# Convolution taps of a Mamba-2 block read from the projection's PSUM bank, with the first decay sums moved to the head of TensorE's slot

## The reference

```python
zxbcdt = x @ W_in                       # z 512 columns, xBC 640 columns, dt 8 columns
lhs = transpose(xBC, (0, 2, 1))         # channels first
conv = conv_general_dilated(lhs, conv_w[:, None, :], padding=[(3, 0)], groups=640)
xBC = silu(transpose(conv, (0, 2, 1)) + conv_b)
# x_ssm, B, C are cut out of xBC; dt = softplus(dt + dt_bias)
def step(s, inp):                       # state, over the tokens
    s = s * dA_t[..., None, None] + dBx_t
    y = einsum('bhpn,bn->bhp', s, C_t)
# y = (y + D * x_ssm) * silu(z), RMS norm, times norm_weight, then y @ W_out
```

## Time and profile before

| | us |
|---|---|
| median of the three runs | 1308.08 |
| profiled execution, its own time | 1312.65 |
| span of the profiled execution | 1310.9 |
| busy TensorE matmul | 1062.4 (81%) |
| busy VectorE | 809.1 (62%) |
| busy GpSimd | 655.7 (50%) |
| busy ScalarE | 618.4 (47%) |

### The profile page before, as it was taken

How to read it: one execution, slowest core, us unless ns; L and a number is a source line. 1 busy time by engine, 2 the same in 40 slices (tenths; PEclk the granted TensorE clock), 3 DMA queues, 4 the chain that set the end, 5 groups by cost and what they waited for, 6 DMA issues and landing times. The chain is left out here.

```text
span 1310.9 us, 21923 instructions
## 1 busy us (share of the span) xinstructions
PE 1062.4 (81%) x6532; PEld 883.3 (67%) x6532; DVE 809.1 (62%) x1611; ACT 618.4 (47%) x1494; POOL 655.7 (50%) x593
## 2 busy tenths in 40 slices
PE   3747999999916788999999999989747999999900
PEld 3646999999914566766666666657536999999800
DVE  6974444444437898698989897875383444444434
ACT  1333555555513565556565656564333555555400
POOL 6913555555421465556565655567505555555300
PEclk9998999999966888788988888899868999999955
DMA  6861222222232111111111100000062222222178
GB/s 230 267 273 49 78 77 77 78 77 78 58 109 73 49 37 41 37 45 35 47 41 42 41 25 17 17 17 25 29 257 65 77 77 78 77 77 76 53 243 275
DMA packets 73242, 112.20 MB, mean 86 GB/s; under 512 B 10664, under 2 KB 60336, under 8 KB 71856
## 3 DMA queue, kind: packets, MB, share of 16 engines
q1 hardware_dynamic: 47888, 58.77, 13.2%
q0 software_dynamic: 13824, 37.77, 8.8%
q10 hardware_dynamic: 11424, 14.30, 3.2%
HBM read 66.76 MB, written 44.04 MB: 85 GB/s over the span
## 5 line engine op out<-in xcount | busy, mean ns | idle before, releaser
L399 POOL DMA_INDIRECT ys_d<-xs,row_of x144 | 142.0, 986 | 195.3 <-DVE xs L779 189.5
L768 DVE TENSOR_TENSOR xl<-pT,xh 128x256 fp32r<-128x256 f32 x144 | 61.1, 424 | 223.9 <-ACT xh L476 223.9
L394 POOL DMA_INDIRECT xs<-xn_d,token_of x144 | 139.8, 971 | 114.4 <-DVE token_of L753 71.2
L463 ACT ACTIVATE hs<-pH 128x512 f32<-128x512 f32 x144 | 86.0, 597 | 233.8 <-PE pH L581 233.8
L773 DVE TENSOR_TENSOR h2l<-hs,h2h 128x512 fp32r<-128x512 f32 x144 | 99.8, 693 | 78.0 <-ACT h2h L471 77.8
L1548 DVE SCALAR_TENSOR_TENSOR acc<-raw,cwh,acc 128x512 f32<-128x512 f32 x104 | 120.9, 1208 | 2.2 <-POOL acc L1075 1.2
L1171 ACT ACTIVATE ex<-bank,dts 128x128 f32<-128x128 f32 x256 | 72.5, 366 | 98.9 <-PE bank L1316 98.9
L601 PE MATMUL pY<-w2h,h2h 128*128 x576 | 102.8, 300 | 0.5 <-DVE h2l L773 0.3
L1060 POOL TENSOR_TENSOR yv<-yv,sz 128x512 f32<-128x512 f32 x32 | 48.0, 1501 | 95.8 <-DVE yv L1598 95.8
L581 PE MATMUL pH<-w1h,xh 128*128 x288 | 92.7, 404 | 1.8 <-DVE xl L768 1.1
L581 PE MATMUL pH<-w1l,xh 128*128 x288 | 92.7, 404 | 0.0
(11 more groups left out here) (248 smaller groups left out, 2668.8 us busy)
## 6 DMA issues: line engine op xcount, KB each, us to landing
m_yg<-ys_d SPq DMA_DIRECT2D x64, 128.0 KB, 2.1
xs<-ys_d SPq DMA_DIRECT2D x16, 512.0 KB, 6.0
wst<-in_L_ffn_w_dram ACTq DMA_DIRECT2D x8, 512.0 KB, 4.7
xs<-in_L_attn_x_dram SPq DMA_DIRECT2D x8, 512.0 KB, 6.6
hs<-in_L_ffn_w_dram ACTq DMA_DIRECT2D x8, 512.0 KB, 5.0
xn_d<-xs SPq DMA_DIRECT2D x8, 512.0 KB, 3.2
lo_d<-w1l SPq DMA_DIRECT2D x1, 4096.0 KB, 11.8
lo_d<-w2l SPq DMA_DIRECT2D x1, 4096.0 KB, 21.3
```

Source lines behind the costliest of these rows:

```text
L394: pool.indirect_dma_start(out=xg[:, t % NX, :], out_offset=None, in_=xn_d, in_offset=bass.IndirectOffsetOnAxis(ap=token_of[:, t:t + 1], ax ...
L399: pool.indirect_dma_start(out=ys_d, out_offset=bass.IndirectOffsetOnAxis(ap=row_of[:, t:t + 1], axis=0), in_=y[:, t % NX, :], in_offset=No ...
L463: act.activation(r[:, u, :], pH[u][:, :], ACT.Relu).then_inc(relu_done.sem, 1)
```

## The change

Nothing is changed outside `mamba_block`.

- `raw` and `tap` are gone, and with them ScalarE's copy of the bank, its two scaled copies per group, GpSimd's `add_tap` and VectorE's `keep_last`. ScalarE writes tap 3 with the bias from the bank to `acc`, and VectorE adds the taps of shift 1, 2 and 3 from the bank, for all five blocks (15 instructions per group).
- The three first columns of a group need the previous group's last three. ScalarE saves these from the bank (`hsave`), GpSimd makes the halo's share of three columns for all blocks in six small chained instructions in slot 2 (`carry`), and ScalarE writes the three first columns of `acc` one at a time with that share as bias (`hc`).
- A projection waits until VectorE has finished the previous block's taps (`taps`).
- The blocks move: early in slot 0 (m = 1) and slot 1 (m = 3); late in slot 3 (m = 0), slot 0 (m = 2) and slot 1 (m = 4). VectorE taps the late ones in the next slot directly after `scale_state`, the early ones after `new_state` in their own slot. Their tanh and silu stand at the end of the slot for m = 0, 2, 4, and at the head of the next for m = 1, 3 (`HANDED`).
- `pX2` and `pLog` move to `pT`, the bank of `turn_xc` and `turn_y`; `turn_x2` waits for ScalarE's copy of this slot's yT.
- `sums(s+1, 0)` moves to the head of TensorE's slot, ahead of `from_state`.

```diff
-PROJECTED = {3: (2, (0, 1)), 0: (1, (2,)), 1: (1, (3, 4))}
-TAPPED = {0: (1, (0, 1)), 1: (1, (2,)), 2: (1, (3, 4))}
+EARLY = {0: (1, 1), 1: (1, 3)}
+LATE = {3: (2, 0), 0: (1, 2), 1: (1, 4)}
+TAPPED = {0: (1, 0), 1: (1, 2), 2: (1, 4)}
+HANDED = {1: (1, 1), 2: (1, 3)}
+HALO = CONV - 1
...
-        pX2, pLog = pP[:, 0:D], pP[:, D:D + E]
+        pX2, pLog = pT[:, 0:D], pT[:, D:D + E]
...
+            def carry(G):
+                u, v = G % 2, (G + 1) % 2
+                pool.wait_ge(h_saved.sem, h_saved.done(G))
+                halo_chain.link(pool.tensor_tensor(hc[:, v, :, :], hsave[:, u, :, :], cwh[:, :, 0:1].to_broadcast([P, NB, HALO]), ALU.mult))
+                halo_chain.link(pool.tensor_tensor(hc[:, v, :, :], hc[:, v, :, :], per_head(cbh[:, :], HALO), ALU.add))
+                for n in range(1, HALO):
+                    w = HALO - n
+                    halo_chain.link(pool.tensor_tensor(ht[:, :, 0:w], hsave[:, u, :, n:HALO], cwh[:, :, n:n + 1].to_broadcast([P, NB, w]), ALU.mult))
+                    last = pool.tensor_tensor(hc[:, v, :, 0:w], hc[:, v, :, 0:w], ht[:, :, 0:w], ALU.add)
...
             def first_taps(G, m):
                 act.wait_ge(p_ready.sem, p_ready.done(B))
-                act.activation(raw[:, b, CONV - 1:], pP[:, :], ACT.Copy).then_inc(raw_done.sem, 1)
-                act.activation(acc[:, q, b, :], raw[:, b, 0:GT], ACT.Identity, bias=cbh[:, b:b + 1], scale=cwh[:, b, 0:1]).then_inc(tap0.sem, 1)
...
+                fresh = G == 0 or not carries(G - 1)
+                if carries(G):
+                    last = act.activation(hsave[:, q, b, :], pP[:, GT - HALO:GT], ACT.Copy)
...
+                if not fresh:
+                    act.wait_ge(h_ready.sem, h_ready.done(G - 1 - (G - 1) * GC // PER))
+                    for n in range(HALO):
+                        act.activation(acc[:, q, b, n:n + 1], pP[:, n:n + 1], ACT.Identity, bias=hc[:, q, b, n:n + 1], scale=cwh[:, b, HALO:HALO + 1])
+                at0 = 0 if fresh else HALO
+                act.activation(acc[:, q, b, at0:GT], pP[:, at0:GT], ACT.Identity, bias=cbh[:, b:b + 1], scale=cwh[:, b, HALO:HALO + 1]).then_inc(tap0.sem, 1)
...
-            def project(G, m, s):
+            def project(G, m):
-                pe.wait_ge(raw_done.sem, raw_done.done(G * NB + m - 1))
-                pe.wait_ge(x2T_copied.sem, x2T_copied.done(s - 3))
-                pe.wait_ge(logit_copied.sem, logit_copied.done(s - 3))
+                pe.wait_ge(taps.sem, taps.done(G * NB + m - 1))
...
             def turn_x2(i, s):
-                pe.wait_ge(raw_done.sem, raw_done.done(blocks_before(s + 1) - 1))
+                pe.wait_ge(yT_copied.sem, yT_copied.done(min(s, T - 1)))
...
             for s in SLOTS:                     # TensorE
+                if live(s + 1):
+                    sums(s + 1, 0)
                 if live(s):
                     from_state(s)
...
                     out_product(s - 1)
-                if live(s + 1):
-                    sums(s + 1, 0)
...
+            def convolve(G, m):
+                b = ORDER[m]
+                dve.wait_ge(tap0.sem, tap0.done(G * NB + m))
                 for n in range(1, CONV):
+                    if n > 1:
+                        dve.wait_ge(tap_chain, tapped[0])
+                    a = acc[:, G % 2, b, n:GT]
+                    ins = dve.scalar_tensor_tensor(a, pP[:, 0:GT - n], cwh[:, b, HALO - n:HALO - n + 1], a, ALU.mult, ALU.add)
...
             for s in SLOTS:                     # VectorE
                     scale_state(s)
+                for B in blocks(s, TAPPED):
+                    convolve(*B)
+                for B in blocks(s, HANDED):
+                    silu(*B)
...
-                convolve(blocks(s, TAPPED))
+                for B in blocks(s, EARLY):
+                    convolve(*B)
```

More of the change, by code:

```diff
@@ L914, in mamba_block @@
             step(n) for n in ("xT", "xT_hi", "xT_lo", "z", "tz", "sz", "dt", "dt_added", "x2T", "x2T_copied", "logit", "logit_copied"))
[L915 to L918, removed]
+        soft, exp_u, a_done, al_done, rest_done, cum_ready, cum_copied, exps, dec_in, dec_out, decdt = (
+            step(n) for n in ("soft", "exp_u", "a", "al", "rest", "cum", "cum_copied", "exps", "dec_in", "dec_out", "decdt"))
+        p_ready, tap0, taps, tb_done, xc_done = (step(n) for n in ("p", "tap0", "taps", "tb", "xc"))
+        h_saved, h_ready, h_chain = step("h_saved"), step("h_ready"), sem("h_chain")
         sm_ready, bt_done, turned, xt_done, e0_ready, ex0_done, e1_ready, ex_done, xdt_done, M_done, xw_done = (
@@ L945, in blocks @@
                 return ()
-            ahead, places = table[s % GC]
+            ahead, m = table[s % GC]
             G = s // GC + ahead
-            return tuple((G, m) for m in places) if 0 <= G < NG else ()
+            return ((G, m),) if 0 <= G < NG else ()
         def rooted(s):
             return live(s + 9) or live(s - 2) or live(s - 1)
-        def blocks_before(s):
-            return sum(len(blocks(n, PROJECTED)) for n in range(-LEAD, s))
         def ends(i):
@@ L1086, in _ @@
                     powers(s + 1)
-                for G, m in blocks(s, PROJECTED):
-                    if m in BY_POOL:
-                        add_tap(G, m)
+                G = s // GC + 1
+                if s % GC == 2 and 0 <= G < NG and carries(G):
+                    carry(G)
         @block.scalar
         def _(act):
-            for s in (al_done, norm_done, norm2_done, x2T_copied, logit_copied, xT_hi, tz_done, exp_u, exps, dec_out, raw_done, tap0, tap_act, tb_done,
+            for s in (al_done, norm_done, norm2_done, x2T_copied, logit_copied, xT_hi, tz_done, exp_u, exps, dec_out, h_saved, tap0, tb_done,
                       xt_done, bt_done, ex0_done, ex_done, sq_done, yT_copied):
@@ L1227, in _ @@
                     tanh(*B)
-                for B in late:
+                for B in blocks(s, LATE):
                     first_taps(*B)
@@ L1380, in _ @@
                     turn_xc(s + 1)
-                for B in first:
-                    project(*B, s)
+                for B in blocks(s, EARLY):
+                    project(*B)
                 if live(s + 1):
@@ L1533, in weigh @@
                 dve.tensor_tensor(row(G, DECDT), row(G, DEC), row(G, DT), ALU.mult).then_inc(decdt.sem, 1)
-            def convolve(pieces):
+            tapped = [0]
+            def convolve(G, m):
+                b = ORDER[m]
+                dve.wait_ge(tap0.sem, tap0.done(G * NB + m))
                 for n in range(1, CONV):
[L1538 to L1564, removed]
+                    if n > 1:
+                        dve.wait_ge(tap_chain, tapped[0])
+                    a = acc[:, G % 2, b, n:GT]
+                    ins = dve.scalar_tensor_tensor(a, pP[:, 0:GT - n], cwh[:, b, HALO - n:HALO - n + 1], a, ALU.mult, ALU.add)
+                    if n == CONV - 1:
+                        ins.then_inc(taps.sem, 1)
+                    else:
+                        ins.then_inc(tap_chain, 1)
+                        tapped[0] += 1
             def silu(G, m):
```

46 lines of the change are left out of this document (20 added, 26 removed).

## The result

| | us | ratio to before, 95% interval |
|---|---|---|
| before, 13 runs | 1307.22 (1304.77 to 1312.86) | |
| after, 13 runs | 1300.50 (1293.54 to 1304.95) | 0.9937 [0.9917, 0.9957] |
| after, in the series of experiments, 12 runs | 1301.41 (1293.63 to 1312.27) | 0.9956 [0.9929, 0.9984] |
| forecast | 1280, a gain of 28 | 0.979 |

The change gains, but some 5 to 8 us and not 28 (5.1 and 6.7 between the medians, 5.8 and 8.2 by the ratios). The kernel after also scatters more than the one before: 11 to 19 us between its fastest and slowest run in a series, against 7 to 11. The kernel before ran again beside each series, with medians from 1306.5 to 1308.1, so times out of different series compare to within some 2 us.

A forecast was written before the change was run, and what follows sets the result against it. Bound: the handshake between VectorE's tail, TensorE's head and the clock. Period 65.4 to 60.4, gain 5.0 times six 30, seventh group 1, last slots -3: 28 in all, 1284.6, or 1280 on the median's scale; range 1256 to 1314.

The forecast's parts named there:

- waits A and B: A: late projection waits for the early block's taps, slots 0 and 1, 1.1 us each; B: `turn_y` in slot 2, 1.8.
- The carry's six instructions: Six chained GpSimd instructions at slot 2's end, once per group: 2 us, hidden, between 0.6 and 5.2.
- The first sums: 0.44 us of TensorE work moved to the slot's head: counted 0, between -0.4 and +0.4 per slot.
- R2: Rival: nothing gained, TensorE meets the new waits at a low clock in all four slots; period 65, 1308 us; chance 0.14.
- R3: Rival: slower, taps keep 1.25 us and all five blocks lie on a path; period 68.4, 1329 us; chance 0.14.
- a gain of less than forecast: Remaining case: 1296 to 1301 us, with `carry` at its dear end or small handshakes in each slot; chance 0.11.
- small handshakes: Allowance of 0.8 us per group, added to 56.1 to give 56.9 at full clock.
- ScalarE, 1.2 us from the bank's arrival to `tap0`: ScalarE's copy of three columns, three single columns and wide pass before the taps: 1.2 us, between 0.9 and 1.4.
- The lead-in slots wait for the first norms, 0: Slots of the lead-in: they wait for the first norms, so the change costs 0 there.
- the loss by low stretches: Clock falls in three slots of four, 1.8 us each; on the path in slots 1 and 3: 3.5 us per group.
- R1: Rival: the new stalls leave the clock at 2.4 GHz; period 56.9, 1259 us; chance 0.16.
- The tail, forecast -3: Last slots: `turn_x2` comes after the copy of yT, ahead of `out_product`, 0.8 us in about four slots: -3.

The follow-up runs named there:

- The run with the second bank: The changed kernel with the first group's blocks m = 1 and 3 projected into the bank `pY`, free before chunk 0: 1297.63 us, 0.9927.

## Why the prediction was wrong in size and right in kind

Right: the direction, and what goes and comes. The taps' rows stand at 748 ns (I took 720), `xTl` is no longer waited for, and waits A and B appear where they were put. Wait B came to the tenth: `turn_y` in slot 2 waits 1.80 us in four of the six groups, forecast 1.8, and in this one starts 741.03 - 730.41 = 10.6 us after the head, forecast 10.7 (TensorE by time, slots 2 and 3). That is in part luck: in the fourth group, without the three one-column instructions, the wait is 1.28, so the forecast, which put ScalarE too low, must have put something else in that run too high.

```profile
730.41 1.12 PE L1260 MATMUL bank<-S,CT 64*128 64x512 f32 x2
741.03 0.82 PE L1345 MATMUL bank<-ident,yv 128*128 128x128 f32 x4 [1.80 <-POOL yv L1057]
758.92 0.41 PE L1415 MATMUL bank<-dts,incl_tri 128*128 128x32 f32 x2 [1.31 <-DVE dts L1531]
```

The carry's six instructions took 1.9 to 2.1 us in GpSimd's free stretch, forecast 2, and GpSimd's product behind them waits for VectorE all the same. The first sums cost nothing in the new order. R2's 1308 lies above the interval, and its period of 65 (its own working, 60.4 and 3 x 1.8, gives 65.8) was 61.0 to 61.8; R3 is out, since no tap took more than 752 ns. What came is the case I gave 0.11 without a name, a gain of less than forecast (1296 to 1301), and of its two causes, a dear `carry` or small waits, the second. The range, 1256 to 1314, held the time.

Wrong: the gain, 28 against 5 to 8. Slot by slot, at full clock (from `from_state` to `from_state`; means over those of the six groups that have no low stretch in that slot, first execution of after):

| slot | forecast | after | without the three one-column instructions |
|---|---|---|---|
| 0 | 13.9 + 1.1 | 16.18 | 15.64 |
| 1 | 13.9 + 1.1 | 15.57 | 14.81 |
| 2 | 10.9 + 1.8 | 12.79 | 12.41 |
| 3 | 13.4 | 15.52 | 15.70 |
| small handshakes | 0.8 | | |
| sum | 56.9 | 60.1 | 58.6 |

1. **The term "ScalarE, 1.2 us from the bank's arrival to `tap0`" failed**, and with it its bounds, 0.9 to 1.4: it is 1.57. The one-column instructions take 352 ns each and follow each other every 240; I took the 177 ns of a plain copy of 8 columns. The wide pass takes 789 ns; I took the plain copy's 598, although the trace of before held the same operation, with bias and scale from tiles, at 816 ns. The line of tap 0 in the kernel before (repeated), 455 to 815 us:

```profile
L1140 ACT ACTIVATE acc<-raw,cbh,cwh 128x512 f32<-128x512 f32 x28 | 22.8, 816 | 0.9
```

   The three instructions cost some 16 us in all, as the run without them shows. The forecast's 1.2 lies half-way between that run's 0.84 and 1.57, so about 8 of the 16 were not in the sum; that half is worked out, not measured.

2. **"The lead-in slots wait for the first norms, 0" failed**: -7 to -8 us in the traces. `pP` now comes free only after ScalarE and three taps, 3.2 us in the lead-in (`hsave` at 417.16 to the last tap's end at 420.35) in place of the copy's 0.6, and in the lead-in too little else stands between two projections to hide it: TensorE waits 1.6 to 3.3 us ahead of each. The run with the second bank undoes it in the trace.

3. **The base.** 65.4 us per group held one group of 71.1; the second execution shows 64.8. That is 0.6 x 6 = 4 us which could not be gained.

4. **Waits left out.** Slot 3 has 2.1 us more than the forecast's 13.4: the cumulative sums wait 1.2 to 1.3 us for VectorE's softplus, some of whose small operations take 1 us beside GpSimd's, and in four of the six groups `turn_y` waits 0.6 to 1.4 for GpSimd there too. Slot 0 has 0.65 for `dts`. Both reach TensorE because it is no longer late itself. No run took them away alone.

5. **The clock, against me.** I put the loss by low stretches at 3.5 us per group; it is 61.0 to 61.8 less 60.1, 1.0 to 1.8. The granted clock was 0.98 (0.96 in the repeat), which is what R1 said, but R1's 1259 did not follow, since its period of 56.9 stands on terms 1 and 4. The errors of 1 and 4 (+3.2) and of the clock (-1.7 to -2.5) nearly cancelled, and so the forecast period of 60.4 looks better than it was.

6. **The tail, forecast -3, is -5.5**: 1.7 us up to chunk 31, and 3.8 behind it, where a low clock stands over the output product. The forecast counted the later `turn_x2` and no clock there. Why the clock is low there stays open: behind chunk 31 the tail takes 24.0 us in both executions of after, 21.0 in the one with the first sums put back, and 20.6 with the last router scores in `pP`.

The account from 28, in the repeated executions: six groups 30 - 4 (base) - 8 (61.8 against 60.4, six times) = 18, seventh group +2, tail -5.5, lead-in -8, gives 6.

## What to carry to other kernels

Cost an instruction by the row of its own form: an activation with bias and scale read from tiles is not a copy, and one column of it costs twice the smallest copy. Before taking an operand straight from PSUM, count the bank's whole turn, from the first matmul to the last reader, and look at the stretch in which nothing hides it (here the first group). Follow a change to the last slots as well as to the first: the clock cost more there than the work that was moved. Take a base period from more than one execution, and measure by leaving the suspect's work out how much of it stands on the path: here taps of nearly no width gave 26 us.

## What the runs showed of the hardware

- Taking one of VectorE's two SBUF operands away sped up both engines. The taps fell from 1254 to 748 ns with 739 as their shortest, and GpSimd's `xD`, code unchanged, from 1368 to 1043 ns. The group of GpSimd's line from 500 to 860 us, first before (repeated), then after:

```profile
L1069 POOL TENSOR_TENSOR xD<-xt,heads 128x512 f32<-128x512 f32 x22 | 30.1, 1368 | 0.0
```

```profile
L1066 POOL TENSOR_TENSOR xD<-xt,heads 128x512 f32<-128x512 f32 x23 | 24.0, 1043 | 0.0
```

  The Trainium skill says in "GPSIMD Engine Reference", section 1, Specifications, that GpSimd shares its SBUF interfaces with VectorE and contends with VectorE instructions that have two SBUF inputs; these rows agree, from both sides. That it is the taps which slow `xD` is borne out by the kernel before with its taps cut to 16 columns: `xD`, in the old order, takes 1043 ns there too.

- For ScalarE the bank was the cheaper source: the same pass over 512 columns took 816 ns from `raw` in SBUF (before) and 773 from PSUM (after). The Trainium skill, "VectorE: DVE Perf Modes", section on the TRN2 errata, gives ScalarE a fixed part of 224 cycles for an SBUF source and 172 for PSUM at 1.2 GHz, 43 ns apart, and the rows show 43. For VectorE it gives PSUM 65 ns more; the taps show 748 from PSUM against 718 for the shortest from SBUF, 30.

- The clock was low (0.50) for 91 and 79 us between 455 and 875 us in the two executions of before, and for 17 and 34 in those of after (stretches added up), though TensorE still waits: 0.6 to 1.8 us at the new places, where the wait for `xTl` had been up to 2.3. I had expected each new wait to bring a low stretch with it; most did not.
